# Preparing the next window's input before the second matrix product, and five accumulator banks instead of seven in the first

## The reference

```python
x = x + 0.5 * ffn(layernorm(x), w1, conv_w, conv_b, w2)
x = x + attn(layernorm(x), slope_rate, qkvu_w, qkvu_b, out_w, out_b, theta)
x = x + 0.5 * ffn(layernorm(x), w1, conv_w, conv_b, w2)

def ffn(x, w1, conv_w, conv_b, w2):
    h = bit_linear(x, w1)              # 1024 -> 4096
    h = depthwise_conv1d(h)            # 3 taps along the sequence, padding 1
    h = silu(h)
    return bit_linear(h, w2)           # 4096 -> 1024
def bit_linear(x, w):                  # both are quantized first
    # activations: s = 127 / max(|x| over features); round(x * s) / s
    # weights: s = 1 / mean(|w|); clip(round(w * s), -1, 1) / s
```

## Time and profile before

| | |
|---|---|
| median of 3 runs | 8805.28 us |
| the profiled execution's own time | 8817.21 us |
| span on its slowest core (core 7) | 8815.7 us |
| spans of the eight cores | 8751.6 to 8815.7 us |
| mean granted TensorE clock | 0.693 to 0.698 of full speed |
| TensorE busy | 3806.7 us (43%) |
| VectorE busy | 3719.6 us (42%) |
| ScalarE busy | 1186.8 us (13%) |
| GpSimd busy | 792.0 us (9%) |
| chain that ended last | DVE 38%, PE 34%, DMA 9%, ACT 9%, issue 6% |

### The profile page before, as it was taken

One profiled execution on the slowest core, in us unless ns is written; L12 is line 12 of the kernel. 1 busy time (PEld: TensorE's weight loads), 2 busy tenths in 40 slices (PEclk: granted clock), 3 DMA queues, 4 the chain that ended last, 5 costly groups with the idle time before them and its releaser, 6 DMA issues.

```text
span 8815.7 us, 52810 instructions; the slowest of 8 cores (8751.6 to 8815.7 us)
## 1 busy us (share of the span) xinstructions
PE 3806.7 (43%) x15718; PEld 1578.8 (18%) x15718; DVE 3719.6 (42%) x6312; ACT 1186.8 (13%) x1870; POOL 792.0 (9%) x739
## 2 busy tenths in 40 slices
PE   0045454434435443355555554333434444353353
PEld 0011111111112111122222221111111121121121
DVE  4453545534463545122222223444345435344533
ACT  0020110202021120011111111111201111210210
POOL 0010102020210102000000000000011022012102
PEclk9967676666667766677766766666666776676676
DMA  3312122132212222300000001111221333332133
GB/s 124 125 38 67 52 68 71 43 81 58 62 38 72 57 62 62 77 5 5 5 5 5 5 5 39 48 48 50 74 72 52 82 81 66 91 86 65 50 100 77
DMA packets 886069, 501.71 MB, mean 57 GB/s; under 512 B 695682, under 2 KB 835266, under 8 KB 882594
## 3 DMA queue, kind: packets, MB, share of 16 engines
q1 hardware_dynamic: 831666, 403.94, 17.3%
q0 software_dynamic: 54128, 94.38, 4.6%
HBM read 424.89 MB, written 83.89 MB: 58 GB/s over the span
## 4 chain that ended last, share of the span: by engine, by line
DVE 38%; PE 34%; DMA 9%; ACT 9%; issue 6%; POOL 2%; another core or an unknown queue 1%; DVEq 1%; ACTq 0%; POOLq 0%; SPq 0%
DVE Rh L562 7%; PE psA L767 5%; DVE bca L641 5%; PE psB L767 5%; PE psD L381 3%; PE psA L920 3%; DVE ar L498 3%; DVE g L521 3%; PE psB L920 3%; ACT g L541 3%; POOL g L554 2%; PE psC L319 1%; DVE bca L430 1%; PE psA L722 1%
## 5 line engine op out<-in xcount | busy, mean ns | idle before, releaser
L554 POOL TENSOR_TENSOR g<-g,bca 128x512 f32<-128x512 f32 (+2 forms) x640 | 710.5, 1140 | 3446.0 <-DVE bca L322 3425.4
L562 DVE TENSOR_SCALAR Rh<-g 128x512 bf16<-128x512 f32 (+2 forms) x640 | 651.6, 1079 | 116.0 <-POOL g L554 104.2
L767 PE MATMUL psA<-Rh,wba 128*128 128x512 bf16 (+2 forms) x2560 | 510.5, 356 | 79.1 <-DMA wba<-wq2s 78.7
L767 PE MATMUL psB<-Rh,wbb 128*128 128x512 bf16 (+2 forms) x2560 | 472.8, 338 | 74.2 <-DMA wbb<-wq2s 70.2
L641 DVE TENSOR_REDUCE bca<-g 128x512 f32<-128x16384 f32 (+2 forms) x20 | 440.8, 22040 | 47.8 <-ACT g L541 40.4
L326 PE MATMUL psC<-rows,onesr 1*128 1x512 f32 (+2 forms) x72 | 67.5, 1035 | 801.9 <-DVE Rh L562 785.7
L541 ACT ACTIVATE g<-g 128x512 f32<-128x512 f32 (+1 forms) x512 | 279.8, 616 | 849.6 <-DVE hedge L534 849.5
L920 PE MATMUL psA<-y,wqh 128*128 128x512 bf16 x1024 | 281.0, 424 | 221.0 <-ACT cosf L871 79.2
L338 PE MATMUL psF<-identf,bca 128*128 128x128 f32 (+1 forms) x132 | 36.3, 425 | 779.3 <-DVE bca L641 648.5
L920 PE MATMUL psB<-y,wqh 128*128 128x512 bf16 x1024 | 260.0, 400 | 94.8 <-ACT uh L937 31.8
L953 DVE COPY vtm<-psT 128x512 bf16<-128x512 bf16 x64 | 27.2, 425 | 634.4 <-PE psT L948 597.5
(11 more groups left out here) (302 smaller groups left out, 6784.9 us busy)
## 6 DMA issues: line engine op xcount, KB each, us to landing
wba<-wq2s SPq DMA_DIRECT2D x80, 1024.0 KB
wbb<-wq2s SPq DMA_DIRECT2D x80, 1024.0 KB
wba<-wq1s SPq DMA_DIRECT2D x64, 1024.0 KB
wbb<-wq1s SPq DMA_DIRECT2D x64, 1024.0 KB
xs<-ar POOLq DMA_DIRECT2D x14, 2048.0 KB, 14.4
wfull<-w1T SPq DMA_DIRECT2D x1, 16384.0 KB
wfull<-w2T SPq DMA_DIRECT2D x1, 16384.0 KB
x4a<-xs SPq DMA_DIRECT2D x8, 2048.0 KB
```

The lines of the kernel that those rows point to most:

```text
L554: vpool = k.rec("gp", lambda e, hc=hc, w=w: e.tensor_tensor(g[:, hc * 512:hc * 512 + w], g[:, hc * 512:hc * 512 + w], bca[:, 0:w], ALU.mul ...
L562: vR = k.rec("ve", lambda e, hc=hc, w=w: e.tensor_scalar(Rh[:, hc * 512:hc * 512 + w], g[:, hc * 512:hc * 512 + w], MAGIC, -MAGIC, ALU.add ...
L767: e.matmul(ob_[:, 0:w], wb[:, hc * 128:(hc + 1) * 128], Rh[:, hc * 512:hc * 512 + w], start=(hc == 0), stop=(hc == HCH - 1)),
```

## The change

`ffn` is reordered, and some buffers are split:

- `xload(wi)` loads x of window wi. Windows 0 and 1 are loaded at the start, and window wi + 2 at the end of window wi, behind LN2. A copy on VectorE takes the last column of each feature chunk into a new tile xedge, which replaces the read from the other x buffer.
- `prep_rp(wi)` does `ln_quant`, or in the second FFN the load of rp. For window wi + 1 it is recorded in window wi, behind the rounding of the hidden tile and ahead of W2. `ln_quant` there works in the first 4096 columns of g instead of ar2.
- The hidden scale and the output scale are broadcast into a new tile hbc instead of bca.
- HB has five banks (psA, psB, psE, psF, psG); psC and psD are left to broadcasts and sums.
- LN2 works in the second 4096 columns of g, in y2sq and y2st (which share the memory of Rh), so that rp and sq are free. Rounding into Rh waits for the store of y2st.
- rows shrinks from 4096 to 3072 columns, and debugging code is gone.

```diff
+    y2st = A("y2st", [128, 4096], BF16, 86 * KB_)
+    y2sq = A("y2sq", [128, 4096], BF16, 94 * KB_)
...
+    def bcast_to(dst, row_ap, w, wait):
...
-    def ln_quant(src, w, rdst, wait, xc_wait=None, sqb=None):
+    def ln_quant(src, w, rdst, wait, xc_wait=None, sqb=None, xcb=None):
...
-        return bcast(rows[0:1, 1024:1024 + w], w, [("sc", vs)])
+        return bcast_to(hbc, rows[0:1, 1024:1024 + w], w,
+                        [("sc", vs), ("ve", k.v("ve"))])
...
+        HB = [psA, psB, psE, psF, psG]
...
+        def xload(wi):
+            sqi, kind, t0, w = wins[wi]
+            xcur = xa if wi % 2 == 0 else xb
+            wt = list(wait0) if wi <= 1 else [("ve", v_xfree[wi - 2])]
+            vx = k.dma("sy", xcur[:].rearrange("p (c t) -> p c t", c=NCH),
+                       _drv(x_src)[:, :, sqi * S + t0:sqi * S + t0 + TT],
+                       wait=wt)
+            v_xload[wi] = vx
+            k.rec("ve", lambda e, xcur=xcur, wi=wi: e.tensor_copy(
+                xedge[:, (wi % 4) * 8:(wi % 4) * 8 + 8].rearrange(
+                    "p (c t) -> p c t", t=1),
+                xcur[:].rearrange("p (c t) -> p c t", c=NCH)
+                [:, :, 511:512]), wait=[("ld", vx)], inc="ve", drain=True)
+
+        def prep_rp(wi, gp_wait):
...
+            if rq_src is None:
+                v = ln_quant(xcur, TT,
+                             lambda ch: rp[:, ch * 512:(ch + 1) * 512],
+                             [("ld", v_xload[wi]), ("te", st8["w1te"])],
+                             xc_wait=[("gp", gp_wait)], xcb=g)
+                v_rpq[wi] = ("ve", v)
+            else:
+                v_rpq[wi] = ("ld", k.dma(
+                    "sy", rp[:].rearrange("p (c t) -> p c t", c=NCH),
+                    _drv(rq_src)[:, :, sqi * S + t0:sqi * S + t0 + TT],
+                    wait=[("te", st8["w1te"]), ("ve", k.v("ve")),
+                          ("gd", k.v("gd"))]))
...
-                HB = [psA, psB, psE, psF, psC, psG, psD]
...
-                    banks = [HB[(cg * 4 + cl) % 7] for cl in range(4)]
+                    banks = [HB[(cg * 4 + cl) % 5] for cl in range(4)]
...
-            vR = round_hidden_grouped(w, vbc)
+            vR, vpool = round_hidden_grouped(w, vbc, rh_gd=st8["y2gd"])
+            vbb_ = bcast_to(hbc[:, 512:1024], rows[0:1, 2560:2560 + w], w,
+                            [("ve", vR)])
+            nx = wi + 1
+            if nx < NW and wins[nx][1] != 2:
+                prep_rp(nx, vpool)
...
+            if wi + 2 < NW and wins[wi + 2][1] != 2:
+                xload(wi + 2)
```

More of the change, by code:

```diff
@@ L181, in build @@
     nc.const_aps.register(BF16, 1.0, onescb[:, 0:1])
-    rows = A("rows", [1, 4096], F32, 8 * KB_)
+    rows = A("rows", [1, 3072], F32, 8 * KB_)
+    hbc = A("hbc", [128, 1024], F32, 20 * KB_)
     bca = A("bca", [128, 1536], F32, 24 * KB_)
@@ L331, in bcast2 @@
             drain=True)
+    def bcast_to(dst, row_ap, w, wait):
+        vt = k.rec("te", lambda e: e.matmul(
+            psC[0:128, 0:w], onesr[0:1, :], row_ap, start=True, stop=True),
+            wait=wait, inc="te")
+        return k.rec("ve", lambda e, dst=dst: e.tensor_copy(
+            dst[:, 0:w], psC[:, 0:w]), wait=[("te", vt)], inc="ve",
+            drain=True)
     def cross_max(src01, w, row_dst, wait):
@@ L423, in ln_quant @@
                 sqb[:, ch * 512:ch * 512 + w],
-                ar2[:, ch * 512:ch * 512 + w], AF.Square),
-                wait=[("ve", vv)] if ch == 0 else None, drain=(ch == 0))
+                xcb[:, ch * 512:ch * 512 + w], AF.Square),
+                wait=[("ve", vv), ("te", k.v("te"))] if ch == 0 else None,
+                drain=(ch == 0))
         vs = k.bar("sc", inc="sc")
@@ L561, in round_hidden_grouped @@
                 hc = h0 + cl
+                wtr = None
+                if cl == 0:
+                    wtr = [("gp", vpool)]
+                    if gi == 0 and rh_gd:
+                        wtr.append(("gd", rh_gd))
                 vR = k.rec("ve", lambda e, hc=hc, w=w: e.tensor_scalar(
@@ L564, in round_hidden_grouped @@
                     g[:, hc * 512:hc * 512 + w], MAGIC, -MAGIC, ALU.add,
-                    ALU.add), wait=[("gp", vpool)] if cl == 0 else None,
-                    inc="ve", drain=(cl == 0))
-        return vR
+                    ALU.add), wait=wtr, inc="ve", drain=(cl == 0))
+        return vR, vpool
     def conv_chunk(c, hb, v_te, isfirst, w):
@@ L666, in ffn @@
             wins.append((sqi, 2, None, 1))
-        v_rpfree = 0
-        v_xfree = 0
+        NW = len(wins)
         wb_free = {id(wba): 0, id(wbb): 0}
         pb_free = {}
[L671 to L678, removed]
+        HB = [psA, psB, psE, psF, psG]
@@ L679, in ffn @@
+        xload(0)
+        if NW > 1 and wins[1][1] != 2:
+            xload(1)
+        prep_rp(0, 0)
         for wi, (sqi, kind, t0, w) in enumerate(wins):
@@ L681, in ffn @@
             xcur = xa if (wi % 2 == 0) else xb
-            xprv = xb if (wi % 2 == 0) else xa
+            gw0 = (t0 if kind == 0 else t0 - 1) if kind != 2 else S - 1
             if kind != 2:
[L684 to L706, removed]
-                HB = [psA, psB, psE, psF, psC, psG, psD]
                 for cg in range(8):
```

84 lines of the change are left out of this document (43 added, 41 removed).

## The result

The changed kernel takes 9159.53 us (median of 8 runs, 9150.58 to 9168.47), the kernel before 8808.46 us beside it (8805.16 to 8819.33): ratio 1.0396, 95% interval 1.0385 to 1.0407. It is slower by 351 us. Its profiled execution has a span of 9154.8 us on core 4 against 8815.7 on core 7 before, 339 more.

The account below looks back on a forecast made before the run. The kernel was taken as bound by a chain of waits, not by any engine's rate. Terms 457 - 166 - 12 + 9 + 20 = +308 us gave 9113 us for the median, 3.5% slower; range 9020 to 9220.

Parts of the forecast that it names:

- windows 2 and 7 of the second FFN: Second FFN: W1 starts at once on prefetched weights, its ScalarE part waits for the y store; -31 us each, -62.
- The ring: W1 stages: with five banks, second and third bank of 112 groups join the chain, 2.35 and 1.73 us each; +457 us.
- The first rival: W1: PSUM reuse is hidden as TensorE idles half the time, ring costs 0; 8656 us; chance 4%.
- the second (a lower clock after the longer pause): W1: second and third bank run at 1.2 GHz too, 3.37 us each, 298 us more; 9411 us; chance 5%.
- The normalization ahead of W2: First FFN: ln_quant delays W2 by 48.6 us a window; net gain 27.6 us in six windows, -166.
- The stall: First FFN, W2's third block: waits 3.5 us for VectorE, plus 1.2 if the clock has fallen; sum 4.7 us.
- The one-column window of the first FFN: First FFN, the one-column window with a successor: 129.3 us from W2 to next W1 becomes about 117; -12 (0 to -17).
- The queue ahead of W2: Second FFN: copy, rq load and W2's weights come in turn with TensorE idle, 12.6 us six times; +76 us.
- Between windows of the second FFN: One rq load gone, -5.0 us in five windows; -4 each in windows 1 and 6; -31 each in 2 and 7.
- The starts: Start of each FFN: x of a second window is loaded before anything begins; +9 us each.
- Window 4: Second FFN: copy of x's last column stands ahead of its work, 20 us for x; 61.9 us becomes 91, +30.
- The third rival: First FFN: weights or x load end late, W1 waits after LN2, rounding not hidden; up to 20 us; 9230; chance 9%.

Follow-up runs that it names:

- the pair of experiments: Changed kernel with seven W1 banks again: 8700.21 us; kernel before with five W1 banks instead of seven: 9289.88 us.

## Why the prediction was right

It gave 9113 us and a range of 9020 to 9220; measured were 9159.53. The forecast of +308 compares with +332 in the mean of the eight cores' spans, +339 between the slowest cores and +351 between the medians. The mechanisms named are the ones that the rows show. Of the 24 us that the mean is off, the largest part, 14, lies in windows 2 and 7 of the second FFN; no other term is off by more than 6, so the sum isn't right by errors that cancel.

- **The ring** was forecast at 457 and is 448 by the stages of the changed kernel, 454 in the kernel before, 452 given back with seven banks; in the mean of the eight cores 453, 459 and 453. That the loss stands alone and doesn't act on the reordering is shown by the pair of experiments, 469 and 469 us by the medians, each with some 30 us on both sides. The second bank was taken at 2.35 us and measured 2.34, the third at 1.73 and 1.71 (2.29 and 1.81 in the mean of the cores). The first rival (no cost) is excluded by both; the second (a lower clock after the longer pause) by the bursts of the changed kernel's profile: in the 105 to 121 that can be timed the first bank takes 3.35 us on average, the second 2.26 and the third 1.73 in every one, against 3.31, 2.38 and 1.74 before.
- **The normalization ahead of W2** was 48.6 us a window and is 49.8; the third block was to start 19.9 us after the first and starts 20.1 later. The stall was the cause named, and the clock did fall in it: its block took 1.6 us longer, where I had taken 1.2. The net gain of 27.6 us a window was 25.4 (451.0 - 298.8 over six), 26.2 in the mean of the cores. Waits for W2's weights, such as the 0.67 us above, are part of what is missing; I did not test that apart. By the earlier trace rows the gain has two sources: 18.1 us of rounding now lie beside W2, and the wait of 15.39 us for y2's store is gone because LN2 no longer writes rp, nor ln_quant ar2. No run separates the two.
- **The one-column window of the first FFN** gained 7 us instead of 12 (9 in the mean), and the last one, for which I had named nothing, lost 4 (3 in the mean).
- **The queue ahead of W2** in the second FFN was mis-sized a little, 13.9 us in place of 12.6 (13.2 in the mean), with the right parts: 5.15 and 5.69 in the chain, and about 1.0 between broadcast and rq.
- **Between windows of the second FFN** lies the step that was off most. Windows 2 and 7 were to gain 31 us each and gained 22 (24 in the mean). The forecast set 13.6 us from W2's last addition to VectorE's first row of W1 against 44.2 before. In the mean of these two windows on all cores it is 19.6, against 44.0: 3 us more for the store of y, which takes 16.0 to ScalarE's first row in place of 13 (14.9 below), and 3 for ScalarE's four rows ahead of VectorE, which the forecast left out. Windows 0, 1, 5 and 6 gave 20.7 in place of 28, but 30.9 in the mean. The slowest core is the exception: W2 of windows 5 and 6 took 65.9 and 63.9 us there, against 58.3 and 57.8 before, with waits for its weights such as this one in window 5:

```profile
8080.84 8.44 PE L793 MATMUL psB<-Rh,wbb 128*128 128x511 bf16 x32 [3.14 <-DMA wbb<-wq2s]
```

- **The starts** were taken at +9 each. The two slowest cores show +1.9 and -0.3, the means +10.5 and +5.7, and moving the copy gave 12.5 back at the first.
- **Window 4** was forecast by the copy's wait, and the wait is there: 17.39 us against 20.
- The third rival, W1 late behind LN2, came up in single windows only: of the 48 (six windows on eight cores) W1 waits over 2 us behind the broadcast in five, 5.1 at most.

ScalarE's wait for the y store in window 3 of the second FFN, from the timeline of the changed kernel:

```profile
7352.83 1.89 PE L753 MATMUL psA<-rp,wba 128*128 128x512 bf16 x8
...
7355.64 0.93 POOL L76 DMA_DIRECT2D y<-ar  x1 [82.14 <-DVE ar L819]
...
7370.50 0.78 ACT L497 ACTIVATE ar<-psA,cb,cw 128x512 f32<-128x512 f32 x1 [144.62 <-DMA y<-ar]
...
7373.46 0.75 DVE L513 SCALAR_TENSOR_TENSOR ar<-psA,cw,ar 128x511 f32<-128x511 f32 x1 [18.46 <-ACT ar L497]
```

W1 runs at once, four banks and one more, and then the group waits 14.9 us from the issue of the store, because conv_group uses ar2 as scratch.

What the time is made of: the first FFN's six windows gain 152 us, nearly all that was forecast, though 49.8 us of each normalization only changed their place and just its rounding is overlapped. The two banks that were set aside for it cost three times as much, and the second FFN, which had nothing to overlap, got the queue's new order as a loss.

## What to carry to other kernels

Code that is recorded ahead of a stage on an in-order engine isn't overlapped with it: pieces have to be placed between the stage's blocks, and each piece's work on the other engines has to fit beside one block (147 us, 102 to 192, here). Before banks are taken from a ring, look at which bank of a group waits for the release; each bank more that waits joins the chain with its own time, the first of them at a higher price while the clock still rises (2.34 us against 1.71 here), and that is paid in every group. Waits on "all that was recorded so far" and copies tied to a load's landing move with the code: after a reordering, ask of each what it now stands ahead of.

## What the runs showed of the hardware that was not expected

In some bursts of W1 the banks are 2.10 us apart instead of 1.73. The windows view with five banks in the kernel before gives the granted clock of such a stretch and of a usual one (length, PE busy, weight loads, DVE, ACT, POOL, clock, DMA share, GB/s):

```profile
915.10:919.00 3.90, 3.90 (x16) 1.60 (x15) 0.61 (x1) 1.55 (x2) 0.00 (x0) 0.81 0.15 23
...
890.60:897.20 6.60, 6.60 (x32) 3.02 (x31) 0.22 (x1) 3.11 (x4) 0.00 (x0) 1.00 0.03 5
```

The clock was 0.81 of full speed in the first and 1.00 in the second, and 2.10 x 0.81 = 1.70. Of 112 third banks of a burst 14 take 2.10 us in that profile, 19 with six banks and 5 in the kernel before; in the changed kernel none of 105 does. So it isn't tied to fewer banks. What brings it about is not shown. The sums over the stages contain it, so it doesn't explain the 15 us by which the median with five banks exceeds them.
